# The short tile's shift of the score differences moves from POOL to ACT

## The reference

```python
energy = jnp.einsum('bqhad,bkhad->bahqk', qd, kd)
energy = jnp.where(causal, NEG, energy)
scores = jax.nn.softmax(energy / np.sqrt(D), axis=-1)
diff = scores[:, 0] - lam * scores[:, 1]
diff = jnp.where(causal, NEG, diff)
diff = jax.nn.softmax(diff, axis=-1)
att = jnp.einsum('bhqv,bvhd->bqhd', diff, v)
```

## Time and profile before

| | before |
|---|---|
| time, median of 3 runs | 2129.94 us (2122.12, 2129.94, 2130.46) |
| profiled execution | 2123.43 us, span 2121.7 us |
| PE busy | 1555.5 us (73%) |
| DVE busy | 1467.3 us (69%) |
| ACT busy | 1219.2 us (57%) |
| POOL busy | 1057.3 us (50%) |

### The profile page before, as it was taken

How to read it: one execution, slowest core, us unless ns; L and a number is a source line. 1 busy time by engine, 2 the same in 40 slices (tenths; PEclk the granted TensorE clock), 3 DMA queues, 4 the chain that set the end, 5 groups by cost and what they waited for, 6 DMA issues and landing times. The chain is left out here.

```text
span 2121.7 us, 44318 instructions
## 1 busy us (share of the span) xinstructions
PE 1555.5 (73%) x10713; PEld 1091.9 (51%) x10713; DVE 1467.3 (69%) x4351; ACT 1219.2 (57%) x3332; POOL 1057.3 (50%) x1477
## 2 busy tenths in 40 slices
PE   0579814347888888988888888888888888886521
PEld 0355402125666666666666666666666566763221
DVE  5774431127887888888888888888888776751167
ACT  0121102126887878887888887788878776761100
POOL 0220003225666667767766777767677565552200
PEclk9999956666878999899999999999999877676655
DMA  3330271111111111111111121111111100000084
GB/s 122 94 87 0 67 245 30 41 39 33 24 28 36 41 48 43 38 51 47 45 48 38 43 52 43 49 43 38 49 48 42 40 20 20 15 15 30 35 324 158
DMA packets 183784, 122.58 MB, mean 58 GB/s; under 512 B 140225, under 2 KB 140609, under 8 KB 183746
## 3 DMA queue, kind: packets, MB, share of 16 engines
q1 hardware_dynamic: 183746, 122.15, 19.6%
HBM read 57.07 MB, written 33.55 MB: 43 GB/s over the span
## 5 line engine op out<-in xcount | busy, mean ns | idle before, releaser
L1185 ACT ACTIVATE ex<-bank,nbias 128x512 f32<-128x512 f32 (+3 forms) x1024 | 527.8, 534 | 141.2 <-DVE nbias L902 140.7
L895 DVE TENSOR_REDUCE nmax<-bank 128x2 f32<-128x1024 f32 (+3 forms) x448 | 340.7, 795 | 29.9 <-PE bank L1331 29.5
L1361 PEld LDWEIGHTS bank<-vs,pr 128*128 128x128 f32 x2560 | 343.2, 210 | 17.8 <-issue 13.4
L1361 PE MATMUL bank<-vs,pr 128*128 (+1 forms) x2560 | 343.4, 286 | 7.2 <-issue 4.1
L1329 PE MATMUL bank<-ks,qs 96*128 (+2 forms) x1024 | 271.8, 342 | 95.7 <-ACT ex L1185 94.2
L1343 PE MATMUL bank<-cst,df 128*128 128x128 f32 x1280 | 274.5, 319 | 88.8 <-ACT pr L1202 88.5
L1081 POOL TENSOR_SCALAR ex<-ex,gam 128x128 f32<-128x128 f32 (+3 forms) x512 | 313.4, 623 | 0.0
L1202 ACT ACTIVATE pr<-bank 128x128 f32<-128x128 f32 (+3 forms) x512 | 233.0, 455 | 70.5 <-PE bank L1343 70.1
L927 DVE CUSTOM_DVE_ANT_0 df<-ex 128x128 f32<-128x128 f32 (+3 forms) x512 | 263.3, 529 | 9.7 <-issue 4.9
L1343 PEld LDWEIGHTS bank<-cst,df 128*128 128x128 f32 x1280 | 174.1, 171 | 117.9 <-ACT pr L1202 101.6
L1185 ACT ACTIVATION_READ_ACCUMULATOR ex<-bank,nbias 128x1 f32 x1024 | 216.6, 212 | 0.0
(11 more groups left out here) (215 smaller groups left out, 3164.0 us busy)
## 6 DMA issues: line engine op xcount, KB each, us to landing
qs<-turned SPq DMA_DIRECT2D x384, 64.0 KB, 2.2
xs<-in_x SPq DMA_DIRECT2D x64, 256.0 KB, 3.0
x_dram<-y SPq DMA_DIRECT2D x32, 256.0 KB, 3.8
b_xs<-x_dram SPq DMA_DIRECT2D x32, 256.0 KB, 2.6
x<-x_dram SPq DMA_DIRECT2D x32, 256.0 KB, 2.7
x_dram<-x SPq DMA_DIRECT2D x32, 256.0 KB, 2.0
y_dram<-scratch SPq DMA_DIRECT2D x32, 256.0 KB, 2.0
c_x<-x_dram SPq DMA_DIRECT2D x8, 1024.0 KB, 13.6
```

What stands on the lines that cost most here:

```text
L895: ins = dve.tensor_reduce(nmax[:, j, i, :], energy(j, i), X, ALU.max, negate=True)
L1185: ac.activation(ex[j % 4][:, a, lo:hi], energy(j, i)[:, a, :], ACT.Exp, bias=nbias[:, j, i, a:a + 1], scale=reg, accum_out=esum[:, j, i, a ...
L1361: mm = pe.matmul(bank[:, 7, t * DV:(t + 1) * DV], pr[j % 2][:, lo + k * P:lo + (k + 1) * P], val, start=(k == 0), stop=(k == t))
```

## The change

POOL's function `shift` and its place in POOL's order (lag 5, first slot of a step) are taken out. ACT's function `shift` takes the tile as an argument, and ACT's third slot of a step, which had the long tile's shift, now has the short one's ahead of it, both with lag 5. ACT announces both.

```diff
-                def shift(at):
-                    j = at.j
-                    dbias_done.wait(gp, at.units(1), apart_p)
-                    lo, hi = span(j, 0)
-                    gp.tensor_scalar(df[j % 4][:, lo:hi], df[j % 4][:, lo:hi], rsum[:, j, 0, 0:1],
-                                     dbias[:, j, 0:1], ALU.mult, ALU.add).then_inc(shifted_short.sem, 1)
...
-                run_bodies(gp, [[(5, shift)], [(2, mask), (2, scale)], []],
+                run_bodies(gp, [[], [(2, mask), (2, scale)], []],
...
-                def shift(at):
-                    j = at.j
-                    dbias_done.wait(ac, at.units(1))
-                    lo, hi = span(j, 1)
-                    ac.activation(df[j % 4][:, lo:hi], df[j % 4][:, lo:hi], ACT.Identity, bias=dbias[:, j, 1:2],
-                                  scale=rsum[:, j, 1, 0:1]).then_inc(shifted_long.sem, 1)
+                def shift(i):
+                    def f(at):
+                        j = at.j
+                        dbias_done.wait(ac, at.units(1))
+                        lo, hi = span(j, i)
+                        ac.activation(df[j % 4][:, lo:hi], df[j % 4][:, lo:hi], ACT.Identity, bias=dbias[:, j, i:i + 1],
+                                      scale=rsum[:, j, i, 0:1]).then_inc((shifted_short, shifted_long)[i].sem, 1)
+                    return f
...
-                run_bodies(ac, [[(7, probs(1)), (0, exps(1)), (0, exps(0))], [(6, probs(0))], [(5, shift)]],
+                run_bodies(ac, [[(7, probs(1)), (0, exps(1)), (0, exps(0))], [(6, probs(0))], [(5, shift(0)), (5, shift(1))]],
```

More of the change, by code:

```diff
@@ L1063, in _ @@
             def _(gp):
-                for s in (rstd_done, rstd2_done, rope_done, masked, scaled, shifted_short, sq_done, ri_done, lo_done,
+                for s in (rstd_done, rstd2_done, rope_done, masked, scaled, sq_done, ri_done, lo_done,
                           rlo_done, al_done, lo2_done):
@@ L1170, in _ @@
             def _(ac):
-                for s in (hi_done, xt_out, rhi_done, v_done, turned_out, exp_done, shifted_long, prob_done, ah_done, at_out, hi2_done,
+                for s in (hi_done, xt_out, rhi_done, v_done, turned_out, exp_done, shifted_short, shifted_long, prob_done, ah_done, at_out, hi2_done,
                           xt2_out, y_out):
```

## The result

| | before | after |
|---|---|---|
| time, median | 2126.03 us (4 runs, 2121.51 to 2130.46) | 2192.9 us (4 runs, 2191.22 to 2203.11) |
| profiled execution | 2123.43 us, span 2121.7 us | 2191.71 us, span 2189.9 us |

The ratio is 1.0325, with a 95% interval from 1.0282 to 1.0368: 66.9 us slower. The prediction had the sign and a size of 26 us; the time lies outside its range.

The account below looks back on a forecast made before the run. The bound was taken to be a chain of waits through DVE, ACT and PE, no single engine. 20.7 us (22 full bodies) plus 5 (ten thinner) made 26 us; set between 2149 and 2156: 2153 us, range 2120 to 2190.

Parts of the forecast that it names:

- The chain: One body of eight pairs, 44.55 us, was to be bound by waits passing between DVE, ACT and PE.
- Absorbed: Rival: ACT's idle time hides the added shifts, under 10 us extra, 2130 to 2140 us; chance 0.17.
- faster: Rival: POOL without its shift stops holding DVE through the shared port, 2105 to 2119 us; chance 0.12.
- The price of a shift: On ACT, from start to start, a short shift costs 0.50 us (256 columns) or 0.39 us (128).
- the signs: Expected in the profile after: ACT busy up 120 to 165 us, its wait for `nbias` down from 69.8 us, among others.
- The three stretches, 1.28 us: Three ACT parts of the body's chain each take one short shift: 0.50, 0.39 and 0.39 us.
- less 0.34: Given back per body where DVE's 0.94 us `nbias` runs beside POOL's L1139: late by 0.55 instead of 0.89 us.
- the net of 0.94: Added time per full body, stretches minus give-back: 0.94 us, over 22 bodies 20.7 us.
- The thinner bodies, 5 us: Ten bodies where ACT has more room: 0.5 us each, between 0 and 1.28, together 5 us.
- The rival: Much slower through the clock: PE waits longer, falls to the lower clock more often, 29 us on the chain, 2182; chance 0.14.
- The removal from POOL at nothing: Taking 256 instructions (147.9 us) off POOL was costed at nothing on the chain, apart from the shared port.

Follow-up runs that it names:

- before with filler: Kernel before plus products that nothing reads on PE, at four places ahead of waits (steps 1, 7, 4 and 6): 2096.67 us, ratio 0.9843.
- after with filler: Changed kernel plus the same unread products on PE at the same four places: 2136.71 us, ratio 1.0045.
- the runs with POOL held back: Changed kernel with POOL waiting for `nbias` at step 2, or at steps 0, 2 and 7: 2198.44 us (1.0325) and 2194.29 us (1.0308).
- the kernel before with holds and filler: Kernel before with POOL waiting for `nbias` of steps 0 and 5, plus unread products on PE: 2092.45 us, ratio 0.9837.

## Why the prediction was wrong

- *The chain*: right. ACT's delays of `ex` and `pr` are on it, PE waits longer, and the waits named in the earlier trace rows grew. Absorbed and faster are both excluded.
- *The price of a shift*: right. Two shifts of a pair with the `pr` behind them, in ACT's timeline of the changed kernel:

```profile
1042.36 1.20 ACT L1188 ACTIVATE df<-df,dbias,rsum 128x128 f32<-128x128 f32 x2
1043.46 0.47 ACT L1197 ACTIVATE pr<-bank 128x384 f32<-128x384 f32 x1
...
1047.03 1.23 ACT L1188 ACTIVATE df<-df,dbias,rsum 128x256 f32<-128x256 f32 x2
1048.13 0.61 ACT L1197 ACTIVATE pr<-bank 128x512 f32<-128x512 f32 x1
```

  From the pair's start to `pr` are 1.10 us at either width. With 0.71 and 0.61 us for the long one the short one holds ACT for 0.39 and 0.49, where 0.39 and 0.50 were forecast. This price by start to start held; the signs by busy time (ACT up by 120 us or more) did not.
- *The three stretches, 1.28 us, less 0.34*: at full clock the body grew by 1.33 us. The give-back did come where it was put (the `nbias` of step 5 is 0.96 us before with filler, 0.44 after with filler), though the 0.94 us of the earlier trace rows stood in only three of five bodies of the kernel before (mean of the 22: 0.64, after 0.45). But it did not shorten the chain by as much: taking all of it away in the kernel before gave 0.26 us. So the net of 0.94 was low by 0.4 us, 9 us in 22 bodies. A wait that I had not priced is DVE's for the third projection, 9.8 us in 16 bodies after and none in the waits view before.
- *The thinner bodies, 5 us*: they took 8.9 us (5.2 + 3.7).
- *Net 0.94 us a full body as the whole of the price, with the clock only among the rivals*: this is the step that failed. The 20.7 us for 22 bodies were 56; at full clock 29 of them are ACT's, and 27 (1.23 × 22) are clock. The rival had the right mechanism, and I gave it 0.14. Its size, 29 us on the chain, came out right by luck: it supposed the clock of the full bodies to fall from 0.94 to 0.88, and it fell from 0.935 to 0.924 in the mean of the 22. What it had not seen is that the same time at the lower level costs more after: 3.3 us of the body for 7.3 us, where before it is 2.1 for 5.9. The earlier trace rows showed waits of 0.70, 1.19 and 0.35 us on PE, and the earlier trace rows a clock of 0.94 that the full bodies already lost; the sum should have been made for a body with its clock.
- *The removal from POOL at nothing*: near the truth at full clock, wrong in the kernel before. Without the shift on any engine it cost 1.7%, though the forecast would have been 0. With filler 0.9% is left against the kernel before with filler (0.9936 against 0.9843), so the clock is a part of it; the rest is open. In the changed kernel the term is small: with POOL's instruction kept the time is the same (1.0281 against 1.0325).
- *What I had not named*: `nbias` of steps 2 and 7 held for 1.0 us more each by POOL's instructions. It looked like the cause, and the runs with POOL held back gave no time back. For the same reason ACT's wait for `nbias` did not go down as the signs had it, but from 69.8 to 71.2 us.

Left open: why the fall in the middle of the body lasts 6.8 us after and mostly 3.4 before is not explained from its parts. It stands among PE's longest waits for ACT, but no run changed only one of these waits, so that they decide it is argued and not shown. The filler's own cost was not measured alone, and the parting into ACT's 1.33 us and the clock's 1.23 rests on its being equal in both kernels. The two fillered kernels differ by 40.0 us in their medians and by 30.4 in the spans profiled, so that ACT's share is known to some 10 us.

## What to carry to other kernels

Where TensorE waits several times in each turn of a loop, price a change in two columns: the turn at full clock, and the time at the lower level, which longer waits raise. Read it by windows cut at the loop's own turns; a window of 200 us hid here that three bodies of five had 0.96 and one 0.89. Before moving work to take a stall away, fill TensorE's waits with products that nothing reads: this alone gave 1.6% here, and a stall that looks like the cause (`nbias`, 1.3 instead of 0.2 us) may give nothing when it is cured.

## What was not expected of the hardware

- The bodies fall into a pattern that repeats with the clock's falls: five lengths before (44.78, 44.70, 44.55, 44.93 and 46.38 us), one length after (47.73), three in the kernel without a short shift (45.72, 46.57 and 47.65, from one first `ex` to the next). The time lost does not look like a smooth function of the waits, and the removal of an instruction that PE was seen to wait for only twice in 256 times made the kernel 1.7% slower.
- A DVE instruction on 128x4 elements, 0.23 us by itself, takes 1.20 to 1.38 us beside a POOL operation with two inputs and ends with it to within 0.03 us. The Trainium skill, page "SBUF — State Buffer", section "Who interferes with whom", has a DVE instruction in a 2-port mode and a GpSimd one block each other for the whole instruction; the trace agrees in that the short one is held to the other's end, while no run shows in which mode `nbias` works. The runs show that lifting this block need not give time back.
- A fall has no fixed price. A body at 0.96 is longer than one at 1.00 by 0.85 us in the kernel before with holds and filler (42.86 to 43.71), by 1.46 in that with filler alone (43.12 to 44.58) and in the changed one with filler by 1.69 (44.45 to 46.14) and, in the body right behind, by 0.87 (45.32).
- The kernel before loses 2.1 us of its mean body of 45.20 to the clock (against 43.12 at 1.00), 4.6%, though PE is idle for no more than 1.2 us at a time in its waits for `pr`. The Trainium skill, page "TensorE: Matmul & The Clock Gate", section "A second HAM failure mode: psum-queue depth-cycling", tells of a kernel whose matmul groups had such small idles between them that the clock went up and down, with a loss of throughput; the trace agrees with the behaviour, and the price is that of the rows above.
